# The setup of a Mamba layer: two convolution halves on GpSimd, softplus as a maximum, rows of C in fp32

## The reference

```
xz = x @ in_proj_w.T;  x_ssm, z = split(xz, 2)        # 256 channels each
xc = causal depthwise convolution of x_ssm, 4 taps, + conv_b
x_act = silu(xc)
delta = softplus(x_act @ dt_proj_w.T + dt_proj_b)
B, C  = split(x_act @ x_proj_w.T, 2)                   # 16 states each
h[t]  = exp(delta[t] * A) * h[t-1] + (delta[t] * x_act[t]) * B[t],   A = -exp(A_log)
y[t]  = sum over the 16 states of h[t] * C[t]
out   = ((y + x_act * D_param) * silu(z)) @ out_proj_w.T
```

## Time and profile before

| | us |
|---|---|
| median of three runs | 1120.21 |
| the three runs | 1117.78, 1120.21, 1376.04 |
| the profiled execution | 1112.98 |
| its span, first to last instruction | 1110.9 |
| busy in it: PE, DVE, POOL, ACT | 929.1, 826.7, 645.9, 621.9 |
| mean granted TensorE clock (1 is full speed) | 0.942 |

### The profile page before, as it was taken

The page is one execution under the profiler, slowest core; times in us unless marked ns, Lnnn a source line. Parts: engine busy times, 40 slices in busy tenths (PEclk is TensorE's granted clock), DMA queues, the critical chain, the costliest instruction groups (busy, mean ns, idle before and its releaser), DMA issues.

```text
span 1110.9 us, 11133 instructions
## 1 busy us (share of the span) xinstructions
PE 929.1 (84%) x2933; PEld 541.3 (49%) x2933; DVE 826.7 (74%) x1175; ACT 621.9 (56%) x1131; POOL 645.9 (58%) x445
## 2 busy tenths in 40 slices
PE   6869975788889957999999999877477787787997
PEld 3324432233347625778888888523123333234775
DVE  4895337999964579566666666596999999975754
ACT  5766676301356644555556556768555555535656
POOL 3030134699851233677777777400999999962773
PEclk9989998799999968999999999998699999998999
DMA  2000120000020004476766766202222232224251
GB/s 81 1 0 1 50 76 17 0 0 1 0 71 1 15 14 100 104 162 152 155 142 148 158 142 148 55 0 43 76 85 85 76 81 79 76 67 96 70 150 38
DMA packets 29929, 78.25 MB, mean 70 GB/s; under 512 B 3969, under 2 KB 13825, under 8 KB 25697
## 3 DMA queue, kind: packets, MB, share of 16 engines
q1 hardware_dynamic: 29888, 77.78, 28.3%
HBM read 75.93 MB, written 1.84 MB: 70 GB/s over the span
## 4 chain that ended last, share of the span: by engine, by line
PE 36%; DVE 14%; ACT 5%; issue 3%; POOL 1%; DVEq 0%; ACTq 0%
PE ps L612 36%; DVE y L3059 4%; DVE g L3059 4%; DVE tmp L2377 2%; DVE g L3015 1%; ACT ps L1394 1%; ACT sq L1394 1%; DVE rstd L2377 1%; ACT g L1394 1%; DVE g L2377 1%; DVE ps L2377 1%; ACT rstd L1394 0%; DVE resid L2377 0%; POOL g L2334 0%; DVE g L3012 0%
## 5 line engine op out<-in xcount | busy, mean ns | idle before, releaser
L612 PE MATMUL ps<-parts 128*128 128x512 f32 x1704 | 416.9, 403 | 17.3 <-POOL parts L2219 4.6
L612 PEld LDWEIGHTS ps<-parts 128*128 128x128 f32 x1704 | 322.2, 190 | 106.5 <-issue 17.8
L612 PE MATMUL ps<-g,arena 128*128 128x512 f32 (+2 forms) x408 | 194.3, 614 | 36.1 <-POOL g L2278 15.1
L1394 ACT ACTIVATE g<-ps 128x512 f32<-128x512 f32 (+1 forms) x216 | 127.1, 596 | 148.7 <-PE ps L612 142.6
L2377 DVE TENSOR_TENSOR ps<-g,ps 128x512 f32<-128x512 f32 x160 | 111.3, 696 | 95.4 <-PE ps L612 74.0
L2229 POOL TENSOR_TENSOR parts<-g,parts 128x512 fp32r<-128x512 f32 x112 | 144.3, 1289 | 59.9 <-ACT parts L1394 57.0
L612 PEld LDWEIGHTS ps<-g,arena 128*128 128x128 f32 (+1 forms) x408 | 77.5, 199 | 145.2 <-issue 88.5
L2334 POOL TENSOR_TENSOR g<-g,arena 128x1024 f32<-128x1024 f32 x48 | 112.6, 2374 | 52.8 <-DVE g L2377 52.8
L1394 ACT ACTIVATE parts<-g 128x512 fp32r<-128x512 f32 (+3 forms) x243 | 125.9, 547 | 22.7 <-DVE g L2377 15.1
L1394 ACT ACTIVATE ps<-g,small 128x512 f32<-128x512 f32 x131 | 89.2, 687 | 86.6 <-DVE g L3059 44.0
L2377 DVE TENSOR_TENSOR g<-ps,g 128x512 f32<-128x512 f32 (+1 forms) x140 | 99.0, 707 | 21.7 <-PE ps L612 5.0
(11 more groups left out here) (224 smaller groups left out, 1191.4 us busy)
## 6 DMA issues: line engine op xcount, KB each, us to landing
g<-coef_scratch SPq DMA_DIRECT2D x56, 512.0 KB, 5.8
arena<-b_scratch SPq DMA_DIRECT2D x48, 256.0 KB, 3.3
g<-in_moe_dram SPq DMA_DIRECT2D x34, 192.0 KB, 4.9
g<-coef_scratch SPq DMA_DIRECT2D x24, 256.0 KB, 5.6
arena<-coef_scratch SPq DMA_DIRECT2D x24, 256.0 KB, 4.3
g<-b_scratch SPq DMA_DIRECT2D x16, 256.0 KB, 3.3
g<-in_rope_dram SPq DMA_DIRECT2D x1, 2048.0 KB, 8.6
g<-in_moe_dram SPq DMA_DIRECT2D x2, 768.0 KB, 7.4
```

Of the source, the lines that this page charges most:

```text
L612: return nc.tensor.matmul(o, lhsT, rhs, start=start, stop=stop, **kw)
L1394: return nc.scalar.activation(o, i, func, **kw)
```

## The change

- POOL does two of the eight convolution halves, (c, i) = (1, 1) and (3, 1), with a multiply by the tap and an addition in place of DVE's multiply-add. DVE does the other six. ACT's silus wait for the one or the other.
- B and C are computed as before, but 32 of their rows are copied by ACT in fp32, straight from PSUM, between the silus, one chunk behind them (`bc_copied`). The bf16 split is gone.
- `spread_c` multiplies these 32 rows in fp32 by a selector in fp32, which POOL makes beforehand from the bf16 one with 16 small copies (`c_row`).
- softplus(v) becomes max(v, ln(1 + exp(min(v, 80)))): DVE adds the bias and clips (`clip_dt`), ACT takes Exp and Ln, DVE takes the maximum with v + bias, read again from PSUM (`deltas`). `dl_ready` now counts halves, up to 8. PE's product of the output weights waits for all of them.
- POOL no longer waits for all of delta before its first product; it waits before the third.
- The last `copy_c` stands one step earlier in ACT's list; at the end PE does `gate_up7(0)`, `out_of(3)`, `router7(2)`, `post6_var(3)`, `gate_up7(1)`.
- The semaphores of two table loads are merged.

```diff
+CONV = [(c, i) for c in range(CHUNKS) for i in range(2)]
+CONV_BY_POOL = [(1, 1), (3, 1)]
...
+        bc_rows = arena[1][0:32, 1024:1024 + T]
-        bc_rows = g[0:96, 12, 0:1536].bitcast(BF16)
+        def c_row(n):
+            return g[0:32, 12, n * P:(n + 1) * P] if n < 12 else arena[1][0:32, 512 + (n - 12) * P:640 + (n - 12) * P]
...
@@ PE @@
-            pe.wait_ge(s["dt_ready"], 2 * CHUNKS)
+            pe.wait_ge(s["dl_ready"], 2 * CHUNKS)
...
-            pe.wait_ge(s["bcp_ready"], CHUNKS)
+            pe.wait_ge(s["setup_pool"], 1)
...
-                mm(ps[:, C_BANK, :], row(step % 16 + 16), bc_rows[:, cols(step // 16)]).then_inc(s["cb_bank"], 1)
+                mm(ps[:, C_BANK, :], c_row(step % 16), bc_rows[:, cols(step // 16)]).then_inc(s["cb_bank"], 1)
...
-            router7(2)
             gate_up7(0)
             out_of(3)
+            router7(2)
+            post6_var(3)
             gate_up7(1)
-            post6_var(3)
             pre7_var(3)
...
@@ ACT @@
+            def bc_copied(c):
+                act.wait_ge(s["bc_bank"], c + 1)
+                f(bc_rows[:, cols(c)], ps[0:32, c, :], ACT.Copy).then_inc(s["b_copied"], 1)
             for c in range(CHUNKS):
...
                 for i in range(2):
-                    act.wait_ge(s["conv_ready"], 2 * c + i + 1)
+                    by_hand = sum(k <= 2 * c + i for k, at in enumerate(CONV) if at in CONV_BY_POOL)
+                    if (c, i) in CONV_BY_POOL:
+                        act.wait_ge(s["setup_pool"], by_hand + 1)
+                    else:
+                        act.wait_ge(s["conv_ready"], 2 * c + i + 1 - by_hand)
                     f(G(i, c), G(4 + i, c), ACT.Silu, bias=W(6, "conv_b", i, i + 1)).then_inc(s["xa_ready"], 1)
+                if c:
+                    bc_copied(c - 1)
+            bc_copied(CHUNKS - 1)
             use_log_exp()
             for c in range(CHUNKS):
-                act.wait_ge(s["bc_read"], c + 1)
-                f(b_rows[:, cols(c)], ps[0:16, c, :], ACT.Copy).then_inc(s["b_copied"], 1)
                 for i in (1, 0):
-                    act.wait_ge(s["dt_bank"], 2 * c + 2 - i)
-                    f(G(10 + i, c), ps[:, 4 * i + c, :], ACT.Relu, bias=W(6, "dt_b", i, i + 1))
-                    chain(f(G(8 + i, c), ps[:, 4 * i + c, :], ACT.Abs, bias=W(6, "dt_b", i, i + 1)))
-                    chain.wait()
-                    chain(f(G(8 + i, c), G(8 + i, c), ACT.Exp, scale=-1.0))
+                    act.wait_ge(s["dt_clipped"], 2 * c + 2 - i)
+                    chain(f(G(8 + i, c), G(8 + i, c), ACT.Exp))
                     chain.wait()
                     f(G(8 + i, c), G(8 + i, c), ACT.Ln, bias=one).then_inc(s["dt_ready"], 1)
...
-            act.wait_ge(s["dl_ready"], CHUNKS)
+            act.wait_ge(s["dl_ready"], 2 * CHUNKS)
...
-                    if step - 2 in BY_POOL:
+                    if step - 2 in BY_POOL and step - 2 < BY_POOL[-1]:
                         copy_c(step - 2)
+                if step - 1 == BY_POOL[-1]:
+                    copy_c(step - 1)
...
@@ POOL @@
-                    pool.wait_ge(s["dl_ready"], CHUNKS)
+                    pool.wait_ge(s["w_loaded"], 7 * 16)
+                    pool.wait_ge(s["tables_loaded"], 32)
+                    for n in range(16):
+                        last = pv.tensor_copy(c_row(n), sel[0:32, 16 + n, :])
+                    last.then_inc(s["setup_pool"], 1)
+                    for k, (c, i) in enumerate(CONV_BY_POOL):
+                        pool.wait_ge(s["setup_done"], SETUP["conv_set"])
+                        pool.wait_ge(s["xs_ready"], 2 * c + 2)
+                        for j in range(4):
+                            window, tap = g[:, 8 + i, cols(c, j)], W(6, "conv", 4 * i + j, 4 * i + j + 1)
+                            if j == 0:
+                                pv.tensor_scalar(G(4 + i, c), window, tap, None, ALU.mult)\
+                                  .then_inc(s["conv_step"], 1)
+                                continue
+                            pv.tensor_scalar(G(6 + j % 2, c), window, tap, None, ALU.mult).then_inc(s["conv_step"], 1)
+                            pool.wait_ge(s["conv_step"], 7 * k + 2 * j)
+                            last = pv.tensor_tensor(G(4 + i, c), G(4 + i, c), G(6 + j % 2, c), ALU.add)
+                            last.then_inc(s["conv_step"] if j < 3 else s["setup_pool"], 1)
+                        if k == 0:
+                            pool.sem_inc(s["conv_step"], 1)
...
+                        if step == 2:
+                            pool.wait_ge(s["dl_ready"], 2 * CHUNKS)
...
@@ DVE @@
+            dve.sem_inc(s["setup_done"], 1)
             for c in range(CHUNKS):
                 dve.wait_ge(s["xs_ready"], 2 * c + 2)
+                halves = [i for i in range(2) if (c, i) not in CONV_BY_POOL]
                 for j in range(4):
-                    for i in range(2):
+                    for i in halves:
...
-                        chain.wait(but=0 if (j, i) == (3, 1) else 1)
+                        chain.wait(but=0 if i == halves[-1] and (j == 3 or len(halves) == 1) else 1)
...
-            def b_and_c(c):
...
+            def clip_dt(c):
+                for i in (1, 0):
+                    dve.wait_ge(s["dt_bank"], 2 * c + 2 - i)
+                    v.tensor_scalar(G(8 + i, c), ps[:, 4 * i + c, :], W(6, "dt_b", i, i + 1), 80.0, ALU.add, ALU.min)\
+                        .then_inc(s["dt_clipped"], 1)
+
+            def deltas(c):
+                for i in (1, 0):
+                    dve.wait_ge(s["dt_ready"], 2 * c + 2 - i)
+                    v.scalar_tensor_tensor(G(4 + i, c), ps[:, 4 * i + c, :], W(6, "dt_b", i, i + 1), G(8 + i, c),
+                                           ALU.add, ALU.max).then_inc(s["dl_ready"], 1)
+                dve.wait_ge(s["dl_ready"], 2 * c + 2)
+                tt(g[:, 6:8, cols(c)], g[:, 4:6, cols(c)], g[:, 0:2, cols(c)]).then_inc(s["du_ready"], 1)
+
+            clip_dt(0)
             for c in range(CHUNKS):
                 if c + 1 < CHUNKS:
-                    b_and_c(c + 1)
-                dve.wait_ge(s["dt_ready"], 2 * c + 2)
-                tt(g[:, 4:6, cols(c)], g[:, 8:10, cols(c)], g[:, 10:12, cols(c)], ALU.add)\
-                    .then_inc(s["dl_ready"], 1)
-                dve.wait_ge(s["dl_ready"], c + 1)
-                tt(g[:, 6:8, cols(c)], g[:, 4:6, cols(c)], g[:, 0:2, cols(c)]).then_inc(s["du_ready"], 1)
+                    clip_dt(c + 1)
+                deltas(c)
             chain.wait()
-            dve.wait_ge(s["bcp_ready"], CHUNKS)
```

More of the change, by code:

```diff
@@ L85 @@
                                    ("zeroed", "rest_ready", "decay_negated", "nam_setup", "wo_read", "setup2",
-                                    "f_setup")) for i, name in enumerate(order)}
+                                    "f_setup", "conv_set")) for i, name in enumerate(order)}
 FR_BANKS = (0, 1, 2, 5)
@@ L245, in sb @@
             return ctx.enter_context(nc.sbuf_tensor(name, shape, dt))
-        names = """w_loaded bools_loaded sel_loaded consts_loaded x_loaded rope_loaded pair_loaded0 pair_loaded1
+        names = """w_loaded bools_loaded tables_loaded consts_loaded x_loaded pair_loaded0 pair_loaded1
             out_stored y_ready x_ready h_ready centred sq_act sq_pool var_ready rstd_ready dve_chain
@@ L257, in sandwich @@
             hid_ready e_done coef_stored row_loaded0 row_loaded1 a_ready xs_bank xs_ready conv_ready
-            xa_ready z_bank z_ready dt_bank dt_ready dl_ready du_ready bc_bank bc_read bcp_ready b_copied
+            xa_ready z_bank z_ready dt_bank dt_ready dl_ready du_ready bc_bank setup_pool conv_step dt_clipped b_copied
             cb_bank b_stored da_ready db_ready hs_done hc_ready hc_pool c_copied sum_done carry_saved
@@ L489, in _ @@
                 if layer == 4:
-                    sp.dma_start(sel[:, :, :], selectors[:, 0:32, :]).then_inc(s["sel_loaded"], 16)
+                    sp.dma_start(sel[:, :, :], selectors[:, 0:32, :]).then_inc(s["tables_loaded"], 16)
                 if layer == 2:
-                    sp.dma_start(g[:, 10:12, 0:T], rope[:, :, :]).then_inc(s["rope_loaded"], 16)
+                    sp.dma_start(g[:, 10:12, 0:T], rope[:, :, :]).then_inc(s["tables_loaded"], 16)
                 if layer == 6:
@@ L509, in _ @@
                         if step == 48:
-                            sp.wait_ge(s["dl_ready"], CHUNKS)
+                            sp.wait_ge(s["dl_ready"], 2 * CHUNKS)
                         if step >= 4:
@@ L1218, in _ @@
             last.then_inc(s["setup_bank"], 1)
-            pe.wait_ge(s["bcp_ready"], CHUNKS)
-            def row(n):
-                return sel_bc[:, n, :]
+            pe.wait_ge(s["setup_pool"], 1)
             def spread_c(step):
@@ L2150, in rotate_q @@
             def rotate_q(c):
-                pool.wait_ge(s["rope_loaded"], 16)
+                pool.wait_ge(s["tables_loaded"], 16)
                 pool.wait_ge(s["q_used"], c + 1)
```

(16 more changed lines are left out.)

## The result

| | us |
|---|---|
| before, median of 17 runs | 1119.22 |
| after, median of 17 runs | 1125.72 (1120.53 to 1128.82) |
| ratio after to before | 1.0068, 95% interval 1.0055 to 1.0082 |
| span of the profiled execution | 1123.9 (before 1110.9) |

The run of 1376.04 us was slow and is not in the ratio. By the ratio the change costs 7.6 us (6.2 to 9.2 us by the interval; the medians are 6.5 apart): no difference at the bound of 2%, and about as much as predicted. How it comes about is not as predicted. The two profiled executions are 13.0 us apart, more than the runs: that of the kernel before, 1112.98 us, lies under the lowest of its 17 runs (1115.04). I cut each into four parts at marks on DVE: the entry (its first instruction after the wait for the last norm of layer 5, 717.29 us before, 719.45 after), the first scan, the last product with C (992.36, 1003.73), the end.

What follows compares the result with a forecast made beforehand. A chain of waits was taken to bound the setup, DVE alone the scan stage. Terms +1.8, +2.2, +1.3, +0.7 sum to +6.0 us: 1119.0 or 1126.2 by anchor, 1123 taken between; range 1109 to 1135.

Steps and rivals of the forecast that it cites:

- Setup: Convolution start to first scan: first scan at 783.4 against 781.59, +1.8 us; without contention -5.6, dearest +6.6.
- the port: Convolution: POOL and DVE alternate one for one at shared SBUF access; without this the sum would be 7.4 us lower.
- the second inflow: Setup: POOL's second inflow, released early, holds the port, so DVE's multiply starts 1.8 us late.
- the table load: ACT in the setup, before the softplus: said to end at 764.8, or 759.2 if undisturbed by the port.
- Rival 5: Convolution: POOL's multiplies cost as much as two-input ones or more; +11 to +15 us, 1124 to 1135; chance 0.1.
- Spreads and clip: Scan stage: fp32 C rows delay DVE at three places, +2.2 us, and the score clip twice, +1.3.
- Rival 2: Scan stage: the spreads are covered while the setup stays even; +1.8 to +2.5 us, 1114.8 to 1122.7; chance 0.2.
- Rival 4: Scan stage: PE becomes the bound, 5.2 us per step at half clock; +22 us, 1142; chance 0.05.
- Tail: Kernel end: router behind the third output product makes DVE's routing start later and holds the add-back; +0.7 us.
- Queues: Setup: SP's earlier stores and loads, and POOL's wait before its third inflow, cost the first scan zero.
- Signs named beforehand: Trace marks: POOL multiplies over 0.62, table load ending 764.8, first scan 783.4, DVE's scan-stage idle growing to about 8 us.

Runs made afterwards that it cites:

- e1: Changed kernel with all eight convolution halves back on DVE, plus two unread POOL multiplies while DVE idles; ratio 1.0048 to the kernel before.
- e3: Changed kernel with POOL's wait for all deltas one inflow earlier, ahead of its second; ratio 1.0063 to the kernel before.
- e9: The changed kernel run and profiled again, unchanged; ratio 1.0081 to the kernel before.
- e4: Changed kernel with PE's order behind the last sum as in the kernel before; ratio 1.0055 to the kernel before.
- e7: Changed kernel with PE's spread of the next C row ahead of the variance before the norm; ratio 1.0133 to the kernel before.
- e5: Changed kernel with convolution on DVE, POOL's delta wait before its second inflow, C as three bf16 parts split by POOL; ratio 0.9934 to the kernel before.
- e8: e5 with ACT's table load right behind the last silu, last two B and C copies among Exp and Ln; ratio 0.9917 to the kernel before.
- e10: e8 with POOL's split of the last chunk moved to step 20 of the scan stage; ratio 0.9870 to the kernel before.
- e6: Kernel before with only the two convolution halves given to POOL; ratio 1.0031 to the kernel before, 1.0048 when repeated.

## Why the prediction came out right, and where it was wrong

The time (1123 said, 1125.72 measured) and the sum (+6.0 said, +7.6 measured) hold, but two terms were off in opposite directions, -2.7 and +6.6 us. That the sum came out near is partly luck. So is the time: 1123 was a choice between two anchors, 1119.0 from the profiled execution, which was quicker than any of the 17 runs, and 1126.2 from the median.

- **Setup, +1.8 said, -0.9 measured.** Mechanism right, size too pessimistic. The restructuring without POOL's halves is worth -4.2 (e1), with the inflow held back as well -6.1 (e1 and e3 added up; I had -5.6). Of that POOL's halves take 3.35 back, by the port and the dear multiplies together, and the second inflow 1.9 (1.8 said), 5.3 in place of my 7.4. DVE ended 35.6 us after the entry, 2.0 sooner than said, since it got 24 instructions done in 22.8 us; POOL 38.4, 6.3 later, since its multiplies cost 1.55 alone and not 0.62. The errors partly cancelled at the table load: it ended 45.3 us after the entry where I had 47.5. Rival 5 had the dear multiplies right and the result wrong: behind POOL's late half PE had queued work and lost only 1.57 and 1.24 us of pause.
- **Spreads and clip, +3.5 said, +10.1 measured.** This step failed. I took +0.64 per row from the step behind a pair of full records; the fp32 spread holds PE 1.05, so +0.83. And I let it count only where PE was late already, holding PE's 5.6 free us of 20 for cover elsewhere. But the added work is 16 x 0.83 = 13.3 us per chunk of about 53, which uses up nearly all of it (5.6 of 20 are 14.8 of 53): PE's idle time in the stage falls from 62 to 14 us. So every extra duty of PE (norm 3 x 1.18, clip 2 x 0.93 more, last row 1.02 more, five small waits, in all 1.36, and 1.31 at the start of the stage) is now paid by DVE. These are 9.1 of the 9.3 us by which DVE's waits grew; the other 0.8 of the 10.1 are DVE's own busy time (208.3 to 209.2). Rival 2 is refuted.
- **Rival 4**, half clock throughout, did not come: the granted clock was 1.00 from 800 to 1000, where PE was busy 193.0 of 200 us. Its core, PE becoming the bound, is what happened, at full clock.
- **Tail, +0.7 said**: +0.6 in e9, but not from the router's place (e4); what it is from stays open. **Queues, zero said**: zero, no wait of DVE or POOL in the setup ended with a transfer.
- **Signs named beforehand:** table load and first scan near 764.8 and 783.4 (764.72, 782.88) were met; DVE's waits at about 8 were exceeded (11.6). POOL's multiplies over 0.62 were no sign of the port: alone they take 1.55 (e1). The absolute positions looked right only because this execution entered 2.2 us late.

## What to carry to other kernels

Price an added operation by the whole queue of its engine, not by the places where it is late now: when the slack of a stage is used up, more of its places become waits (3 behind PE before, 12 after), and taking one away (e7) only moves it. Before dividing elementwise work between VectorE and GpSimd, find one row of the same instruction on GpSimd alone and one of both at work. And compare profiles from a common mark ahead of the change; two profiles of one kernel differed here by 3.1 to 3.4 us in the stage alone.

## What the runs showed of the hardware

- GpSimd's multiply of 128x512 by a column of scalars took 1.55 us with nobody in its way (e1), while its product of two 128x1024 tensors takes 2.37, 1.19 per 512. The Trainium skill, GPSIMD Engine Reference, section 4.1 (Engine selection), calls one-input work on GpSimd roughly line-rate; for this instruction, with its column of scalars, the trace does not agree.
- GpSimd and VectorE did not always take turns. In e5 GpSimd's rounding of 96x512 stood beside VectorE's additions for 7.01 us, until the convolution was over, and VectorE was not slowed (4.06 for six additions); with VectorE idle it takes 0.61 (e8 and e10 have the 7.01 too; why the turns of e6 do not come here was not tested):

```profile
745.14 7.01 POOL L2346 CAST g<-arena 96x512 bf16<-96x512 f32 x1 [17.32 <-ACT arena L1397]
...
747.62 4.06 DVE L3064 SCALAR_TENSOR_TENSOR g<-g,arena 128x512 f32<-128x512 f32 x6
...
756.08 0.61 POOL L2346 CAST g<-arena 96x512 bf16<-96x512 f32 x1
```

- An fp32 matmul of only 32 rows costs PE no less than one of 128 rows: 1.05 us to the next record, against 0.96 for the D product (872.90 to 873.86).
- With the kernels unchanged, PE's clock took different courses. In the changed kernel it came back one sum earlier or later at the start of the stage (wait 1.31 or 4.41). In the kernel before it fell in the middle of the stage in both profiles, but to a mean of 0.91 in 860 to 880 in one and 0.83 in the other.
